# Landing waits between table gathers in a fused eight-layer kernel, and two gathers moved at either end

## The reference

```python
x = x + tanh(g_xattn[0]) * L0_xattn(...)   # layer 0: top-2 mixture of 8 experts, routed by the context
x = x + tanh(g_ffn[0])   * L0_ffn(...)     # layer 1: 8-bit feed-forward
x = x + tanh(g_xattn[1]) * L1_xattn(...)   # layer 2: block attention, 16 heads
x = x + tanh(g_ffn[1])   * L1_ffn(...)     # layer 3: argmax choice of 8 component products
x = x + tanh(g_xattn[2]) * L2_xattn(...)   # layer 4: mLSTM with position table:
#   pos_emb = rpe[hops]                    #   hops: [128, 128] integers, rpe: [2017, 128]
#   k_hop   = einsum('bhvc,vmhc->bhvm', qh, pos_emb)
...                                        # layers 5 to 7: experts, slot attention, ternary feed-forward
```

## Time and profile before

| | |
|---|---|
| three runs | 881.66, 885.04, 885.18 us (median 885.04) |
| profiled execution | 886.06 us, its span 884.2 us |
| busy in the span: TensorE, VectorE, ScalarE, GpSimd | 691.8, 566.3, 526.3, 311.7 us |
| GpSimd's table gathers | 128, 125.3 us busy, 979 ns each |
| GpSimd's row gathers and result gathers | 46 and 32, 1058 and 948 ns each |
| moved by DMA | 36.11 MB, mean 41 GB/s |

### The profile page before, as it was taken

The page is one execution under the profiler, slowest core; times in us unless marked ns, Lnnn a source line. Parts: engine busy times, 40 slices in busy tenths (PEclk is TensorE's granted clock), DMA queues, the critical chain, the costliest instruction groups (busy, mean ns, idle before and its releaser), DMA issues.

```text
span 884.2 us, 13703 instructions
## 1 busy us (share of the span) xinstructions
PE 691.8 (78%) x5039; PEld 462.4 (52%) x5039; DVE 566.3 (64%) x1081; ACT 526.3 (60%) x1074; POOL 311.7 (35%) x303
## 2 busy tenths in 40 slices
PE   5479849158788897205998899999799999888977
PEld 4268728023345443102555876666478878665632
DVE  5679816257667663002999557886799424666777
ACT  5656613226657563002568448767488658999867
POOL 4666653734756654770000000001898004000000
PEclk8589958569989797556999899999899999999998
DMA  9335722200001001220300000006000000000001
GB/s 312 103 97 159 99 62 66 54 24 24 22 25 29 26 26 35 52 53 14 37 8 1 1 1 1 1 1 241 0 2 1 1 1 1 1 1 1 1 0 48
DMA packets 40273, 36.11 MB, mean 41 GB/s; under 512 B 21800, under 2 KB 30256, under 8 KB 40208
## 3 DMA queue, kind: packets, MB, share of 16 engines
q1 hardware_dynamic: 33616, 21.73, 8.4%
q0 software_dynamic: 6592, 13.51, 6.9%
HBM read 30.11 MB, written 5.11 MB: 40 GB/s over the span
## 4 chain that ended last, share of the span: by engine, by line
PE 55%; another core or an unknown queue 13%; DVE 13%; ACT 13%; issue 3%; DMA 1%; SPq 0%; POOL 0%; ACTq 0%; DVEq 0%; POOLq 0%
PE ps L1340 4%; PE ps L1553 3%; PE ps L1590 3%; PE ps L427 2%; PE ps L2059 2%; PE ps L2323 2%; PE ps L2010 2%; PE ps L996 2%; PE ps L1581 2%; ACT big L2379 2%; PE ps L1571 2%; PE ps L1013 2%; PE ps L212 2%; PE ps L768 2%
## 5 line engine op out<-in xcount | busy, mean ns | idle before, releaser
L1486 POOL DMA_INDIRECT pe<-in_rpe,idx x128 | 125.3, 979 | 44.2 <-issue 34.0
L1949 POOL TENSOR_SCALAR big<-big,wcols 128x256 f32<-128x256 f32 x1 | 0.9, 939 | 207.7 <-DMA big<-in_l3f_w 207.7
L520 ACT ACTIVATE pe<-ps,wcols 128x256 f32<-128x256 f32 x92 | 37.8, 479 | 35.7 <-remote 17.1
L383 POOL DMA_INDIRECT pe<-normed_rows,pe x46 | 48.7, 1058 | 27.8 <-issue 9.4
L1195 ACT ACTIVATE small<-ps 128x512 f32<-128x512 f32 x16 | 9.5, 597 | 75.2 <-remote 62.3
L1256 DVE TENSOR_TENSOR big<-ps,small 128x512 f32<-128x512 f32 x16 | 10.9, 684 | 66.4 <-ACT small L1196 66.4
L427 PE MATMUL ps<-big 128*128 128x256 f16 x276 | 40.3, 299 | 14.6 <-issue 8.5
L1202 ACT ACTIVATE big<-ps 128x1024 f32<-128x1024 f32 x32 | 32.7, 1022 | 26.7 <-PE ps L993 23.1
L1693 ACT ACTIVATE big<-ps,small 128x128 f32<-128x128 f32 x128 | 34.8, 383 | 17.4 <-PE ps L1581 17.4
L1222 DVE TENSOR_REDUCE small<-ps 128x16 f32<-128x1024 f32 x32 | 38.7, 1217 | 9.7 <-PE ps L987 7.1
L1340 PE MATMUL ps<-nT,big 128*128 128x512 f16 x192 | 44.5, 379 | 0.0
(11 more groups left out here) (428 smaller groups left out, 2059.3 us busy)
## 6 DMA issues: line engine op xcount, KB each, us to landing
pe<-in_l2f_w SPq DMA_DIRECT2D x16, 256.0 KB
tile_results<-big SPq DMA_DIRECT2D x23, 128.0 KB
pe<-in_xrow SPq DMA_DIRECT2D x4, 512.0 KB, 3.8
big<-in_l0x_w SPq DMA_DIRECT2D x8, 256.0 KB
pe<-in_rpe,idx POOLq DMA_INDIRECT x128
cT<-in_cT SPq DMA_DIRECT2D x2, 512.0 KB, 5.3
nT<-in_l0x_w SPq DMA_DIRECT2D x4, 256.0 KB
vx<-in_l0x_w SPq DMA_DIRECT2D x4, 256.0 KB
```

The costliest lines, as they stand in the source:

```text
L383: pool.indirect_dma_start(out=xg16[:, i % RX, h, :, :].rearrange("p r n -> p (r n)"), out_offset=None, in_=xrows_d, in_offset=bass.Indirec ...
L520: ins_ = act.activation(hid32[:, i % RF, f, :], hidden_ps(i, u)[:, f % 2, :], ACT.Relu, bias=wcols[:, bass.ds(at + (COL_AT["l0x_b1"][0] + ...
L1486: pool.indirect_dma_start(out=pe[:, v * D:(v + 1) * D], out_offset=None, in_=ins["rpe"], in_offset=bass.IndirectOffsetOnAxis(ap=idx[:, v:v ...
```

## The change

Two gathers move from the tail to the front (`EARLY` 14 to 16) and two from the tail to later (`IN_L0` becomes 28, so 12 remain in the tail; `IN_L1` becomes 36, which leaves 47 for the last run). A new helper `pool_landed(pool, g)` makes GpSimd wait until all of group g is in memory. It is called at each first gather of a group, for the group just before it, in the tail (but not at v = 16) and in the last run. The wait for `pv` ahead of the last run is gone. The loops of three gathers a step get no such wait, and neither do the result gathers.

```diff
--- before.py
+++ after.py
@@ -383,6 +383,8 @@
                     pool.indirect_dma_start(out=xg16[:, i % RX, h, :, :].rearrange("p r n -> p (r n)"), out_offset=None, in_=xrows_d,
                                             in_offset=bass.IndirectOffsetOnAxis(ap=gidx[:, g:g + 1], axis=0)).then_inc(s_xg[i % RX], 16)
             for v in range(EARLY, IN_L0):
+                if v > EARLY and v % VG == 0:
+                    pool_landed(pool, v // VG - 1)
                 pool_gather(pool, v)
             for k in range(RY):
                 pool.wait_ge(s_ys[k], 16 * len(range(k, NT, RY)))
@@ -1180,8 +1182,9 @@
                     pool_queries(pool, b + 2)
                 if b in KEYS_IN:
                     pool_keys(pool, POOL_KEYS[KEYS_IN.index(b)])
-            pool.wait_ge(A2["pv"], B - 2)
             for v in range(IN_L1 + PER_STEP * (B - 1), S):
+                if v % VG == 0:
+                    pool_landed(pool, v // VG - 1)
                 pool_gather(pool, v)
 
         def act_queries(act, c):
@@ -1473,9 +1476,9 @@
             return ap.rearrange("p (f j) -> p f j", j=VG)
 
         QR = 4
-        EARLY = 14
+        EARLY = 16
         PER_STEP = 3
-        IN_L0 = EARLY + 16
+        IN_L0 = EARLY + 12
         IN_L1 = IN_L0 + 8
         qhalf = big[:, 0:QR * NH2 // 2 * S].rearrange("p (r n) -> p r n", r=QR)
 
@@ -1485,6 +1488,9 @@
                 pool.wait_ge(s_pos[g % 2], 16 * VG * (g // 2))
             pool.indirect_dma_start(out=pe[:, v * D:(v + 1) * D], out_offset=None, in_=ins["rpe"],
                                     in_offset=bass.IndirectOffsetOnAxis(ap=idx[:, v:v + 1], axis=0)).then_inc(s_pos[g % 2], 16)
+
+        def pool_landed(pool, g):
+            pool.wait_ge(s_pos[g % 2], 16 * VG * (g // 2 + 1))
 
         def pool_layer4(pool, link):
             pool.wait_ge(M0["w16"], E)
```

## The result

The changed kernel took 825.3 us (median of four runs, 821.8 to 827.7) beside 883.4 us for the kernel before in the same comparison (880.9 to 885.2): a ratio of 0.934, 95% interval 0.929 to 0.939. The forecast was 827.0. The profiled execution took 827.5 us with a span of 825.7, which is 58.5 less than the span before.

A forecast was written before the change was run, and what follows sets the result against it. Finished TensorE work is reported late, and issue crawls, while GpSimd's gathers run back to back. Tail 13.3 plus last run 44.5 give 57.8 us off 886.06, so 828.3; the runs' median is 1.0 lower, so 827; range 812 to 856.

The forecast's parts named there:

- rival A: Whole kernel: the forecast itself, 827 us; 812 with no residue, 843 with twice the residues; chance 0.58.
- The landing wait: GpSimd's queue, tail and last run: each wait costs 0.9 us, upper bound 2.25, from 2.1 us to land.
- The tail: Tile loop's tail: of the 17.0 us stall, 2.5 and 1.2 us stay, so 13.3 us are gained.
- the 0.6 us: Cost of one run of four gathers, from TensorE's tile cadence of 3.45 us beside it against 2.85 next.
- Two in front at price 0: Before the first row gather: two more gathers take 2.5 of GpSimd's 3.71 us idle, price 0.
- The last run: Last table gathers: 54.7 us stall and 1.5 for low clock returned, 5.1 and 6.6 lost: 44.5 us gained.
- Nine in a row: Six gathers plus v = 81 to 83, ahead of the first landing wait: engines held to 340.9, 5.1 us lost.
- The result gathers: The 32 result gathers, given no waits: their own 25.96 us stall stays.
- The signs to look for: Gaps about 1.2 us, no unknown-queue piece over 6 us between 320 and 400, L1195's longest remote wait under 6.
- B: The 13 new runs of four: each holds reports until it ends, costing 2.56 us; 853 us, chance 0.26.
- C: Last run: breaks do not free the other engines, the stall lasts as long as the gathers; 895 us, chance 0.10.
- D: Tail and last run: landing waits never hold GpSimd, so the runs stay unbroken; 883 us, chance 0.06.

The follow-up runs named there:

- second execution: The changed kernel unaltered, run once more beside the kernel before: 824.3 us, ratio 0.934, span 819.1 us.
- last run alone: Kernel before plus only the landing waits at v = 84, 88 to 124: 766.4 us (1.0056) where the kernel before takes 761.9, 835.5 us (0.944) where 883.8.
- each eighth: Changed kernel with a landing wait at every eighth instead of every fourth gather of the last run: 867.4 us (849.8 to 867.8) beside 883.8.
- results and nine too: Changed kernel plus waits at v = 76 and 80 and seven among the 32 result gathers: 809.3 us (0.909) beside 883.8, 787.3 us (1.0314) beside 761.5.

## Why the prediction was right

The time (825.3 for 827.0), the sign and the mechanism, rival A, are borne out on the chip it was made for. That the time is met within 2 us is in part luck, since several terms are off and cancel. By its own steps:

- **The landing wait.** Priced at 0.9 us with 2.25 as the bound. The gaps measure 1.73 to 1.94 us where 0.30 stood: 1.43 to 1.64 a wait. The term was too small by about 0.6, eleven times, and in the tail, where the two gaps are 3.28 and 2.09, by 2.1 and 0.9. The second execution has gaps up to 3.72 in the last run. The step that failed is the time to land, taken as 2.1 us from the traffic: in the variants' chains it is 2.5 us or more from a gather's start until GpSimd goes on. It did no harm, since the tail had 5.99 us in hand (the wait for the stores) and the last turn of positions starts at 429.8, and no turn waited for a transfer. In the variants with more waits it did harm, as the 27.8 us show.
- **The tail.** 13.3 us forecast. The result gathers start 11.74 us earlier (145.89 to 134.15) although the row gathers start 1.57 later (32.86 to 34.43): 13.3 us. Of this sum, 1.2 us left for two runs of four rest on the 0.6 us, which the quick chip does not bear out.
- **Two in front at price 0.** GpSimd's idle time before the first row gather fell from 3.71 to 2.63, not by 2.5, and the row gather came 1.57 us late. This step failed, by 1.6 us: the cover ends when VectorE releases the gather, and the release itself came later. With sixteen in front that gather starts at 33.9 to 34.6 in all four traces of chips with late reports, and at 32.7 to 33.5 in the traces of quick chips; with fourteen it is 32.6 to 33.1 on both. So the longer unbroken series in front seems to delay that release only where reports are late; how it does so is not shown.
- **The last run.** 44.5 forecast. From the start of its six preceding gathers to layer 3 it is 87.8 us before (328.60 to 416.4) and 42.1 after (315.55 to 357.6): 45.7. Two terms were mis-sized and cancel. Nine in a row were to add 5.1 us to the 3.4; they left 8.09 + 3.73 = 11.8, so they added 8.4 (in the second execution 2.70 + 5.21 = 7.9, so 4.5). The eleven runs of four were to cost 6.6 us, and after 334.1 cost nothing visible: layer 3 lasts 59.0 us with them beside it and 58.5 without. That is the bound of 0 which the text names, and the 0.6 us behind the term was a misreading, as shown above. The 1.5 us for the low clock did not come back as such: the stall that is left has its own low clock, a granted 0.50 from 328 to 334 and 0.68 from 335 to 340.
- **The result gathers.** "Stay" was forecast; a piece of 18.3 us stays where 26.0 stood, and in the second execution 30.3. The stretch from the first result gather to the six gathers ahead of the last run is only 1.3 us shorter (182.7 to 181.4). With it the gain adds up: 11.74 + 1.31 + 45.75, less 0.3 from layer 3 on, are the 58.5 us.
- **The signs to look for.** No unnamed piece over 6 us between 320 and 400: there was one of 8.1, at the nine, the place that the text names. The gaps were to be about 1.2 us and are 1.8. The longest wait for "remote" of L1195 under 6 us: it is 9.0 (L1198 after the change).

Against the rivals: B (each run of four holds reports to its end, 853 us) is out, since no pieces of 2 to 3 us stand at the groups; but its mechanism is real at eight in a row. With four in a row a report is still up to 1.4 us late, 2.7 in the last run alone. C (breaks do not help, 895) would have had one piece as long as the run. D (the waits never hold, 883) falls with the gaps.

What the forecast could not know from one trace is that the stall comes with the chip that runs the kernel. What it says of finished work, that it "is reported late, and issue crawls, as long as gathers run back to back", is true of two of the four comparisons and false of the other two. That the forecast was compared where it holds is luck too: on a quick chip the change would have measured 1.003. The Trainium skill, page "SBUF — State Buffer", section "Who interferes with whom", says that DMA never contends with a compute engine. On the quick chips TensorE runs undisturbed beside unbroken gathers (47.70 of 50 us), and this agrees. On the other chip the same gathers hold its reports for 10 us and more, and breaks give the time back; there the measurement decides against what the forecast drew from the rule, that breaks give nothing back. Whether the gathers and TensorE's reports meet at a memory port, of which that section speaks, or elsewhere, no run here shows.

## What to carry to other kernels

An unnamed wait of one core in the chain, with GpSimd starting indirect transfers one after the other beside it, is a place to break that series after four; eight was too many, and nothing between was tried on purpose. Look at the semaphore first: where the count changes long after the matmul that raises it, the report is held. Give each break its price from the trace, here 1.5 us on GpSimd's queue and 3 to 6 right behind other gathers, and spend them only where the series stands beside work of the other engines and where its last transfer is not yet due, because with a few more of them that queue became the bound. And measure on more than one chip: the change is worth 6.6% in two comparisons and costs 0.3% in a third.

## What was not expected of the hardware

The same kernel takes 883.4 and 883.8 us in two comparisons and 761.9 and 761.5 in two others, with 0.5 to 1.1% from the lowest to the highest run within each, and what is between them lies ahead of layer 3 alone, where GpSimd's gathers run. GpSimd's own pace is alike on both (0.94 us busy and 0.30 idle for each gather); only what the other engines do beside it differs. The records differ as well: of the 2048 steps by which the table gathers raise their two semaphores as they land, the traces of the quick chips hold 2003 to 2037, that of the kernel before 669, and those of its variants beside late reports 785 (each eighth) to 1170 (results and nine too). More breaks, more records; whether the missing records and the late reports have one cause is not shown. No run here shows what about the chips, or the times at which they ran, makes the difference.
